# Layer norm without its shift, an additive mask for the pooled scan, beta and relu by edge group, edge scaling in PSUM, and the pooled scaling between two gathers

## The reference, cut to what matters

```python
# first layer: x1 = LN(x + L0(x)); layer_norm(h, g, b) = (h - mean) / sqrt(var + eps) * g + b
edge_features = x[src] * (1.0 + softplus(coeff_raw) * edge_weight[:, None])
pooled = relu(layer_norm(edge_features @ pool_w + pool_b, ln_pool_g, ln_pool_b))
aggregate = maximum(segment_max(pooled, dst), 0.0)
h = concatenate([x, aggregate], axis=-1) @ final_w + final_b
x1 = _layernorm(x + relu(layer_norm(h, ln_final_g, ln_final_b)))
# second layer: out = LN(x1 + L1(x1)), relational, 8 bases, mean over the edges of a node
agg_b = segment_sum(comp[edge_type, b] * x1[src], dst) / max(degree, 1)
out = _layernorm(x1 + concatenate([agg_0 .. agg_7, x1]) @ weight.reshape(-1, 128) + bias)
```

## Time and profile before

| | us |
|---|---|
| median of 3 runs | 904.17 (903.48 to 909.07) |
| the profiled execution, its time | 903.88 |
| the profiled execution, its span | 902.1 |
| PE busy | 771.0 (85%) |
| DVE busy | 779.1 (86%) |
| ACT busy | 609.9 (68%) |
| POOL busy | 713.0 (79%) |

### The profile page before, as it was taken

How to read it: one execution, slowest core, us unless ns; L and a number is a source line. 1 busy time by engine, 2 the same in 40 slices (tenths; PEclk the granted TensorE clock), 3 DMA queues, 4 the chain that set the end, 5 groups by cost and what they waited for, 6 DMA issues and landing times. The chain is left out here.

```text
span 902.1 us, 18562 instructions
## 1 busy us (share of the span) xinstructions
PE 771.0 (85%) x4588; PEld 566.9 (63%) x4588; DVE 779.1 (86%) x2823; ACT 609.9 (68%) x2862; POOL 713.0 (79%) x702
## 2 busy tenths in 40 slices
PE   5798999999999999999999988888369999987960
PEld 3576777777777777777777876767234544443430
DVE  6988999999999999999999988987259999998870
ACT  3798999999999999999999876766401111111120
POOL 2577889989889988888889577777677777777777
PEclk9989999999999999999999999999879999999995
DMA  4366676666666666666666422235168788878611
GB/s 115 110 220 199 203 227 208 206 213 204 200 215 205 196 215 207 196 215 201 197 213 200 150 85 85 88 99 209 46 216 303 285 306 321 289 287 318 219 66 45
DMA packets 88575, 175.46 MB, mean 194 GB/s; under 512 B 16715, under 2 KB 34023, under 8 KB 82198
## 3 DMA queue, kind: packets, MB, share of 16 engines
q1 hardware_dynamic: 71286, 144.02, 46.7%
q0 software_dynamic: 15744, 29.71, 11.0%
q10 hardware_dynamic: 1440, 0.56, 0.3%
HBM read 105.88 MB, written 70.88 MB: 196 GB/s over the span
## 5 line engine op out<-in xcount | busy, mean ns | idle before, releaser
L704 ACT ACTIVATE junk<-ps 128x128 bf16<-128x128 f32 x884 | 235.3, 302 | 30.2 <-PE ps L554 17.3
L704 ACT ACTIVATION_READ_ACCUMULATOR junk<-ps 128x1 f32 x884 | 206.9, 236 | 0.0
L656 PE MATMUL ps<-agg_all,w_cen 128*128 128x512 f32 (+1 forms) x400 | 179.0, 602 | 1.5 <-DVE agg_all L1185 0.9
L406 POOL DMA_INDIRECT x_dst<-in_x,dst_i x98 | 150.8, 1539 | 20.5 <-issue 7.1
L551 PE MATMUL ps<-w_cen,xT 128*128 128x128 f32 x984 | 161.2, 296 | 0.0
L436 POOL TENSOR_TENSOR work<-work,vec_raw 128x512 f32<-128x512 f32 x98 | 127.7, 1303 | 35.3 <-DVE work L1084 34.7
L551 PEld LDWEIGHTS ps<-w_cen,xT 128*128 128x128 f32 x984 | 130.9, 199 | 29.1 <-issue 29.1
L1185 DVE TENSOR_TENSOR agg_all<-coefs,ps 128x1024 f32<-128x1024 f32 x98 | 117.6, 1210 | 26.2 <-PE ps L642 18.3
L1084 DVE SCALAR_TENSOR_TENSOR work<-ps,st,vec_raw 128x128 f32<-128x128 f32 x492 | 137.8, 343 | 0.4 <-ACT st L719 0.3
L1016 DVE BATCH_NORM_STATS2 bn<-work 128x6 f32<-128x128 f32 x492 | 135.2, 280 | 1.2 <-DVE st L1004 0.6
L406 POOL DMA_INDIRECT x_table<-agg_all,scat_i x98 | 103.3, 1054 | 36.8 <-issue 27.4
(11 more groups left out here) (139 smaller groups left out, 1374.7 us busy)
## 6 DMA issues: line engine op xcount, KB each, us to landing
coefs<-coef_line SPq DMA_DIRECT2D x49, 1024.0 KB, 7.2
rows<-in_x SPq DMA_DIRECT2D x97, 256.0 KB, 2.9
x_table<-work SPq DMA_DIRECT2D x97, 256.0 KB
out_rows<-outb SPq DMA_DIRECT2D x97, 256.0 KB
x_dst_table<-x_dst SPq DMA_DIRECT2D x98, 64.0 KB
rows<-x_dst_table SPq DMA_DIRECT2D x24, 256.0 KB, 2.8
same_prev<-mask_line SPq DMA_DIRECT2D x7, 224.0 KB, 4.3
x_dst<-in_x,dst_i POOLq DMA_INDIRECT x98, 4.0
```

What stands on the lines that cost most here:

```text
L406: return pool.indirect_dma_start(*args, bounds_check=last_node, oob_is_err=False)
L656: last = pe.matmul(MT[b][:, 0:n * D], w_cen[:, W_BASE + m, :], prod[:, b, m, 0:n, :].rearrange("p t d -> p (t d)"), start=(m == 0), stop=( ...
L704: last = nc.scalar.activation(junk[:, kind * CH + m, :], bank[:, cols(m, m + 1)], ACT.Square, accum_out=power[:, b, 1, TOP + kind * CH + m ...
```

## The change

- **No shift in the layer norm.** `x1` is no longer made with mean zero: `means` (L1072) and its semaphore `dve_m` go, ACT's three blocks are a copy with a scale, DVE's one a `tensor_scalar`. The root weights and the bases lose their column means instead, so that a constant in a row of `x1` has no effect on them; for the bases this takes two products with ones (`base_column_sums`) and two DVE operations (`bases_without_mean`) at steps 118 to 121.
- **Root bias.** ACT's copy of `x1T` adds nothing; the bias comes as a 512-column three-row product (`root_bias`) ahead of the four root products.
- **Additive mask.** A line of 0 and -3e38 in bf16 (`apart`) is made at the start, stored, and loaded seven tiles at a time in 14 broadcasts into two slots; the scan is state = max(mask + state, value). The byte mask, still needed by the last stage, is loaded from step `EDGE_ORDER` on.
- **Beta and relu by edge group.** The beta product (L567) goes. ACT adds beta (now one per partition) with relu over a whole group of the line (512 columns, `aggregates`) at the start of each edge group's step, and sets `agg_ready`, for which the first layer waits.
- **Edge scaling in place.** For edge groups L1084 and L1103 write into `H`, and L1030 reads `H`; TensorE waits for that reading (`dve_v`) before it writes the bank again.
- **Pooled scaling between gathers.** On POOL the order per step is beta, gather of destinations, scaling, gather of sources.
- **Order on TensorE.** Up to `EDGE_ORDER`: `turned`, root bias, `rooted`, first bias, first layer, rows, pooled. After it: rows, first bias, first layer, `turned`, pooled, root bias, `rooted`.
- **SP.** The store of `x_dst` goes one step earlier.

```diff
+            def apart_load(k):
+                need(sp, S["dve_scan"], (k - 1) * APART_TILES)
+                part = slice(k * APART_TILES * P, (k + 1) * APART_TILES * P)
+                sp.dma_start(apart[:, k % 2, :], apart_line[:, part].broadcast_to([P, APART_TILES * P])) \
+                    .then_inc(apart_in[k % 2], 16)
...
-                k = c - 4
+                k = c - EDGE_ORDER
...
-                if is_tile(c, 0):
-                    t = c - LATE
+                if is_tile(c, -1):
+                    t = c + 1 - LATE
...
                     gather_dst(t)
-                    need(pool, S["pe_a"], s)
-                    gather_src(t)
                 if is_tile(s, -1):
                     if s + 1 == LATE:
                         pool.wait_ge(S["e_ready"], 1)
                     scale_src(s + 1 - LATE)
+                if is_tile(s, -3):
+                    need(pool, S["pe_a"], s)
+                    gather_src(s + 3 - LATE)
...
+                def root_bias():
+                    if is_group(c, 6):
                         if is_dense(c, 8):
                             pe.wait_ge(S["dve_o"], s - 7)
                         elif c >= 8:
                             pe.wait_ge(S["act_o"], s - 7 - DENSE)
+                        pe.matmul(Y[b], ones3[:, :], root_bias3[:, :], start=True, stop=False, skip_group_check=True)
...
+                        need(pe, S["dve_t"], s - 2)
+                        if is_group(c, 3) and not is_dense(c, 3):
+                            pe.wait_ge(S["dve_v"], s - 2)
+                        pe.matmul(H[1 - b], ones3[:, :], bias3[:, :], start=True, stop=False, skip_group_check=True)
...
+                def pooled_turned():
+                    if is_tile(c, 4):
+                        pe.wait_ge(S["dve_scan"], s - LATE - 3)
+                    if is_tile(c, 2):
+                        pe.wait_ge(S["dve_te"], s - LATE - 1)
+                    if is_tile(c, 3):
+                        pe.wait_ge(S["dve_te"], s - LATE - 2)
+                        pe.transpose(PT, pooled[:, 1 - b, :], ident[:, :]).then_inc(S["pe_cp"], 1)
...
                 if c < EDGE_ORDER:
                     turned()
+                    root_bias()
                     rooted()
...
+                    first_bias()
+                    first_layer()
+                    rows_turned()
+                    pooled_turned()
+                    pooled_layer()
+                else:
+                    rows_turned()
+                    first_bias()
+                    first_layer()
                     turned()
...
-                        nc.scalar.add(x1T[:, 1 - b, :, :].rearrange("p c d -> p (c d)"), VT, 1.0).then_inc(S["act_c"], 1)
+                        nc.scalar.copy(x1T[:, 1 - b, :, :].rearrange("p c d -> p (c d)"), VT).then_inc(S["act_c"], 1)
...
-                            last = nc.scalar.activation(x1_tile(c - 4, m), hn[:, (c - 4) % SLOTS, m, :], ACT.Identity,
-                                                        bias=st[:, 3, TOP + m:TOP + m + 1],
+                            last = nc.scalar.activation(x1_tile(c - 4, m), hn[:, (c - 4) % SLOTS, m, :], ACT.Copy,
                                                         scale=st[:, 7, RES + m:RES + m + 1])
...
+                def aggregates():
+                    if is_group(c, 0) and not is_dense(c, 0):
+                        d = c - DENSE
+                        upto = min((d + 1) * CH, TILES)
+                        act.wait_ge(S["dve_scan"], min(upto + 1, TILES))
...
+                        line = agg_line[:, d * CH * P:upto * P]
+                        nc.scalar.activation(line, line, ACT.Relu, bias=edge_beta[:, 0:1]).then_inc(S["agg_ready"], 1)
...
-                        dve.scalar_tensor_tensor(h, h, 0.0,
+                        dve.scalar_tensor_tensor(h, h if is_dense(c, 3) else H[1 - b], 0.0,
...
-                        dve.tensor_tensor_scan(agg_line[:, bass.ds(t * P, P)], same_prev[:, bass.ds(t * P, P)],
-                                               PT, before, ALU.mult, ALU.max).then_inc(S["dve_scan"], 1)
-
-                def means():
+                        dve.tensor_tensor_scan(agg_line[:, bass.ds(t * P, P)],
+                                               apart[:, t // APART_TILES % 2, bass.ds(t % APART_TILES * P, P)],
+                                               PT, before, ALU.add, ALU.max).then_inc(S["dve_scan"], 1)
...
-                            last = dve.scalar_tensor_tensor(hn[:, (c - 2) % SLOTS, m, :], H[b][:, cols(m, m + 1)],
+                            h = H[b][:, cols(m, m + 1)]
+                            last = dve.scalar_tensor_tensor(hn[:, (c - 2) % SLOTS, m, :] if is_dense(c, 2) else h, h,
...
-                            last = dve.scalar_tensor_tensor(x1_tile(c - 4, m), hn[:, (c - 4) % SLOTS, m, :],
-                                                            st[:, 7, RES + m:RES + m + 1],
-                                                            st[:, 3, TOP + m:TOP + m + 1].broadcast_to([P, D]),
-                                                            ALU.mult, ALU.add)
+                            last = dve.tensor_scalar(x1_tile(c - 4, m), hn[:, (c - 4) % SLOTS, m, :],
+                                                     st[:, 7, RES + m:RES + m + 1], None, ALU.mult)
```

197 lines of the change are left out of this document (115 added, 82 removed).

## The result

| | before | after |
|---|---|---|
| median, us | 904.55 (4 runs, 903.48 to 909.07) | 895.09 (4 runs) |
| ratio to before | | 0.9876, 95% interval 0.984 to 0.9912 |
| profiled execution: time, span | 903.9, 902.1 | 894.1, 892.3 |
| ScalarE's copy to `xT` starts: step 12, 20, 98 | 65.8, 109.0, 485.8 | 62.1, 99.9, 468.7 |
| dense step, 20 to 98: median, mean | 4.808, 4.831 | 4.724, 4.729 |

Three of the four executions of after took 891.5 to 896.05; the fourth was disturbed (1257.71): it counts in the median, which is 894.12 without it, and not in the ratio. The forecast was 878, in 868 to 896. The direction was right and the median lies just inside the range, but about a third of the gain came.

A forecast was written before the change was run, and what follows sets the result against it. A latency loop through TensorE, ScalarE and VectorE, 4.81 us a step, was taken as the bound. Dense steps 17 us, start 3 and edge stage 7, less 1, made 26 us: 878 us, in 868 to 896.

The forecast's parts named there:

- Parts 2 and 3: Dense steps: dropping L567 takes 0.16 us off the loop, dropping L1072 0.08, a one-source L1116 0 to 0.06.
- Part 1: Dense steps: the root bias product adds 0.51 us to TensorE's own step, which becomes 4.59.
- Part 4: Dense steps: loop falls below TensorE's 4.59 us; ScalarE's late squares add some; step 4.61 (4.58 to 4.66), from 4.81.
- Part 5: GpSimd in dense steps: with the scaling between the gathers its row takes 4.65 us at most, hidden by the step.
- The sum: Whole kernel: 87 steps x 0.20 = 17 us; with 3 and 7, less 1, 26 us saved.
- Part 6: Scan, mask loads, byte mask's move, earlier x_dst store and the bases' column sums were all put at nothing.
- Part 7: Steps where edge groups enter, 490 to 516 us: TensorE's net added work counts in full, +0.8 us over five steps.
- Part 9: Start: TensorE multiplies before it turns rows, so waits for ScalarE's copy go; -3 us (0 to -6).
- Part 8: Edge stage: 98 scatters follow each other on GpSimd and end the stage; shorter scatters give -7 us (-10 to +1).
- A: Rival, dense steps: source gather holds L1116 to its end; step 4.76, saving 4 in place of 17, 891 us; chance 0.13.
- C: Rival, dense steps: late squares or a second switch eat the gain; step 4.78, 894 us; chance 0.14.
- B: Rival, dense steps: L1116 waits until L436 ends, 1.47 us more; step 6.08, about 1008 us; chance 0.07.

The follow-up runs named there:

- e16: The kernel after without any root bias product; 976.8 us, ratio to before 1.0025.
- e9: The kernel before with only the edge groups' scaling done in place in PSUM; 899.33 us, ratio to before 0.9953.
- e12: The kernel after without the bases' column sums and the two VectorE operations on them; 891.23 us, ratio to before 0.9863.
- e10: The kernel after with SP's coefficient line stores a step later, behind the next load of rows; 888.71 us, ratio to before 0.9833.
- e1: The kernel after with GpSimd's order of before: both gathers in a row, then the scaling; 987.18 us, against 971.4 for e3.
- e7: The kernel after with GpSimd's scaling right behind beta, ahead of both gathers; 972.52 us, ratio to before 1.000.
- e15: The kernel after with GpSimd scaling one column of the source rows in place of 128; 965.35 us, ratio to before 0.9898.
- e18: The kernel after with line stores a step later, base sums after the edge groups and GpSimd's scaling behind beta; 882.98 us, ratio to before 0.9765.
- e17: Same as e18, but with the edge groups' scaling written to SBUF; 886.43 us, ratio to before 0.9796.
- e3: The kernel after with the byte mask loaded from step 4 on, as before; 971.4 us, ratio to before 1.0032.
- e4: The kernel after with edge groups scaled into SBUF, without TensorE's wait for the residual; 954.19 us, ratio to before 0.9822.

## Why the prediction was wrong, step by step

- **What bounded the kernel before**: the loop was right, and its waits are in the trace (VectorE for L754 19.0 us in 69 steps, as above). What failed is the step behind it. I gave TensorE, ScalarE and GpSimd a length of their own, old and new, and VectorE none. Its row had only 0.43 - 0.28 = 0.15 us of slack in a step, so any lengthening of it by more than what the change takes off would show.
- **Parts 2 and 3, terms removed**: sizes right. L1197 takes 0.27, and the next instruction starts 0.20 behind it, in 0.20 to 0.26; three L802 take 1.00. L567 was on the loop through TensorE, which isn't the longest chain any more; L1072 and L1116 are on VectorE's row and count.
- **Part 1**: 0.51 us right (L545 to L551 0.32, gap 0.17), on TensorE only; e16 shows that it is hidden in the dense steps.
- **Part 4, the step of 4.61**: this is the step that failed in the dense stage. It measured 4.72 to 4.73. The term that isn't there is VectorE's own row with L1090 held for 0.29 beside a gather, which part 5 brings about by its new order; the late squares of ScalarE, from which 4.61 came, set nothing in after.
- **Part 5**: "The step of 4.61 hides it" failed. GpSimd does follow (its beta starts 0.09 behind L1166), and x_dst's gather stayed at 1.59, as said. But I asked only whether its row fits, and not what its order does to VectorE: it removes one hold (L1116's and L1197's, up to 1.45 each) and makes another, 0.29 in every step.
- **The sum**: 20 to 98 gave 8.0 of 15.6. The kernel before has long steps early on, two of them L1116's holds; with them gone the steps from 12 to 20 gave 5.4 where 1.6 was counted. So up to step 98 the forecast missed by 3 us only, and 3.3 us of what made up for the rest is the luck of one profile (e9).
- **Part 6**: of its "at nothing", the scan, the `apart` loads and the x_dst store show no cost. The base sums cost some 2.0 us (e12). And the rows' loads did come late, behind the line store and, in after, the mask; the store alone accounts for 6.0 us (e10). The wait for `line_made` on SP was in the code and in no term.
- **Part 7**: +0.4 for +0.8. **Part 9**: -3.7 for -3. **Part 10**: 0, right.
- **Part 8**: the step that failed in the edge stage is "follow each other on POOL and end the stage", +6.9 us measured for -7. That the scatters become shorter, and by how much, was right, -6.6 for -7. But they had 9.4 us of waits in 140, and I took the other 130 as theirs; e9 shows that 6.2 us off the scatters yield 1.0, and in after the waits for `x1` are 25.8.
- **Rivals**: A's mechanism came, but not at the source gather and not in every step: five blocks held by a gather or a scatter, 1.0 us in all; in the steady steps L1197 takes 0.27 beside the end of L435. C's time nearly came (894), for another reason. B's mechanism came in e1 and was already in before; it was kept off in after by POOL's order. My ground against it, "DVE's own queue fixes the order", didn't protect: in e1 the block started 0.36 before beta, at its usual place, and was held all the same. And that "today's L1116 [...] was not held" is right for gathers only: by the scaling it was held, twice.

The section of the Trainium skill that the prediction weighed (SBUF — State Buffer, "Who interferes with whom") says that a `tensor_scalar` can enter a mode that shuts GpSimd out, and that whoever is first blocks the other. The trace agrees in part: of the ten blocks of after that start well inside a gather or scatter five are held to its end and five are not, and the two-input L1116 of before never took over 0.36 beside a scatter. The section also says that a DVE instruction with two SBUF inputs contends with a GpSimd instruction that reads SBUF. The trace agrees: L1079 in e7 and L1116 in before have two, and ended with GpSimd's `TENSOR_TENSOR`. By the section a block lasts for the one instruction; the trace shows more, 1.72 us through two of them (L1196 and L1116). I had looked for holds by gathers only. What no row explains is why L1090, in after, is held before the scaling has begun and let go 0.23 us before the gather ends, and why with one column queued behind (e15) its hold is 0.08 at most.

## What to carry to other kernels

Before pricing a change, write down the own row of every engine, the one that waits now above all: here VectorE's had 0.15 us of slack in a step, and I hadn't asked. Then test each link of a loop: where an instruction starts just before the end of the one ahead on its own engine, the engine has not stood idle, however near another engine's end lies. And look for one instruction with two lengths; what runs beside it when it is long is part of its price. When a unit that "ends the stage" is to become faster, add up what it would wait for at its new pace; the idle time that it has now is a bound on nothing. And in a program written out by hand, a store that waits for its data delays every load queued behind it.

## What the runs showed of the hardware

- A small DVE operation with two SBUF inputs takes 0.47 us instead of 0.17 while GpSimd's gather runs with a 128-column `TENSOR_TENSOR` queued behind it; with another gather queued (e1, e7, and before) 0.17. In e1 it is held beside the source gather, ahead of the scaling, and never beside the destination gather.
- An `x1` block of DVE that starts with GpSimd's scaling is held through the beta queued behind it: 1.72 us for 0.28 or 0.34.
- A one-source `TENSOR_SCALAR` of DVE that starts during a gather or scatter can be held to its end: 0.32 to 0.72 us for 0.27, five of ten times in after. A two-input `SCALAR_TENSOR_TENSOR` of the same size took 0.34 or 0.35 beside scatters in before.
- Two kinds of chips give the same program 904 and 970 us. The dense steps are equal; the edge stage and the last stage differ, and in place against SBUF comes out 3 us better (e18 against e17) on the one kind and 17 worse (e3 against e4) on the other. What differs in the chips stays open.
